# A pipelined first mixer and router, and expert weights streamed per tile as the stationary operand, in a two-layer Flamingo block

## The chip, the cores and the metric

One Trainium2 chip; the kernel runs on one of its cores. The metric is the device time of one execution in microseconds (us). All tensors are float32 unless a row says bf16 or f16.

## What is computed

The input is 2 x 1024 tokens of width 256. Two layers, each a mixer and a mixture of experts, each added to the residual stream behind a tanh gate:

```python
x = x + tanh(g_xattn[0]) * depool_mixer(layernorm(x), ctx)      # rmsnorm, x @ W_in.T + b_in, plus depooled context rows
x = x + tanh(g_ffn[0])   * experts0(layernorm(x))               # 8 experts, top 2, relu, hidden 1024
x = x + tanh(g_xattn[1]) * attention(layernorm(x), ctx)         # 16 heads, 77 context + 1024 own keys
x = x + tanh(g_ffn[1])   * experts1(layernorm(x))               # 32 experts, top 4
# experts1, token t, chosen expert e:
g = x @ w1[e]; u = x @ w3[e]                                    # 256 -> 192
out[t] += weight[t, e] * ((silu(g) * u) @ w2[e])                # 192 -> 256
```

## The kernel before, in words

The residual stream (16 tiles of 128 tokens) stays in SBUF. The program is a sequence of stages, each a block with a program per engine; a block ends only when every engine's program has ended, SP's included. The stages are `prepare`, `depool_mixer`, `router(0)`, `route(0)`, `experts0`, `combine(0)`, then `project_qkv`, `attend`, `project_out`, `router(1)`, `route(1)`, `experts1`, `combine(1)`.

**First mixer and router.** `depool_mixer` takes 16 tiles in turn. For each, ACT normalises it (L552), PE turns it by two transposes (L534), ACT copies the turned tile out of PSUM (L559), PE multiplies by the input weights and adds the context rows with a one-hot matmul (L543, L544), DVE adds the result to the residual (L517), makes a later tile's one-hot (L510) and takes statistics (L522). When all 16 tiles are through, `router(0)` starts: the statistics of all tiles become a scale and a shift (`moments`, L107 to L114, then L605, L585, L586), and each tile is normalised (ACT, L602), stored to HBM for the later gathers (SP, L621), turned (PE, L635), copied (ACT, L615), multiplied by the router weights (PE, L644) and biased (DVE, L592). SP also loads the small weights and the first five of the eight 1 MB W2 matrices during the mixer; the other three and b2 are issued in `route(0)`.

**route(0)** finds the two experts of each token, the softmax weights, and where every token goes. PE and ACT first turn 19 weight blocks that later stages need (`later_turns`, L869 and L742: the attention weights, the second gate, and b1). ACT's exponential for the softmax (L745) stands behind those 19 copies in ACT's program, and DVE waits for it at L801.

**project_qkv** loads early weights of the second experts from POOL's queue: 26 DMAs of 384 KB (W1 and W3 of two experts each, L1553), behind one memset (L1376). **project_out** issues the rest from SP: W1 and W3 of the last six experts (12 DMAs, L1553) and 30 W2 matrices (L1547), 192 KB each. So at the start of `experts1` W1, W3 and W2 of all 32 experts lie in SBUF.

**experts1** runs 95 tiles of up to 128 gathered tokens of one expert. A tile is gathered by POOL's indirect DMA into a ring of four (L901), turned by PE (two transposes, L1109), copied by ACT (L1160). The turned tokens are then the stationary operand and [W1 | W3] is the moving one: two accumulating matmuls of 384 columns (L1115). ACT takes the silu (L1172), DVE multiplies (L1203), giving tokens x 192; PE turns that in two halves of 96 (L1121), ACT copies it (L1166), and two matmuls with 96 contraction rows and 256 columns give the output (L1130), which DVE copies (L1191) and SP stores (L1220). In iteration j, PE does gate and up of tile j, turns the hidden rows of j-1, does down of j-2, and turns the tokens of j+2. A float32 matmul is two records in the trace.

`experts0` (39 tiles) has the other order already: W1 is streamed per tile (1 MB from SP, L969, its expert number read by SP at L966) and is the stationary operand of 16 matmuls of 128 columns (L992).

Of the kernel before, what the change touches and what calls it, by code (L numbers as in the profile page):

```python
# [27 lines left out]
IH = I1 // 2  # L28
# [26 lines left out]
W2_1 = E1 * W13_BYTES  # L55
ARENA = W2_1 + E1 * 2 * D * 4
# [3 lines left out]
W2_TOP = (TOP - W2_1) // (2 * D * 4)  # L60
EARLY = 26
ATT0 = EARLY * W13_BYTES

# [53 lines left out]
def make_env(nc, ctx, a, out):  # L117
# [15 lines left out]
    e.w0_in, e.w13_early, e.w13_in, e.w2_in = (ctx.enter_context(nc.semaphore(n)) for n in ("w0_in", "w13_early", "w13_in", "w2_in"))  # L133
# [62 lines left out]
    e.w13 = carve(0, [E1, DK, 2 * I1])  # L196
    e.w2b = carve(W2_1, [E1, 2, D])

# [258 lines left out]
W2_EARLY = 5  # L457
# [10 lines left out]
def later_turns(e):  # L468
# [8 lines left out]
    turn.append((raw.b1[0:E0 * HK0, :], E0 * HK0, e.b1T))  # L477
# [3 lines left out]
def depool_mixer(e):  # L481
# [5 lines left out]
    U = 4  # L487
    LAG = 3
    xn = e.carve(0, [U, D], base=e.scr)
    xT = e.carve(U * D * 4, [U, DK, P], base=e.scr)  # L490
    oh = e.carve(2 * U * D * 4, [U, P], base=e.scr)

    with nc.Block() as block:
        @block.sync
        def _(sp):
            load_small(e, sp)
            for ex in range(W2_EARLY):
                load_w2_first(e, sp, ex)

        @block.vector  # L500
        def _(dve):
# [12 lines left out]
            for i in range(NTILE + 1):  # L514
                if i < NTILE:
                    dve.wait_ge(mixed_raw, i + 1)
                    v.scalar_tensor_tensor(e.x[:, i, :], ps[:, U + i % U, 0:D], e.tg[:, 0:1], e.x[:, i, :], ALU.mult, ALU.add).then_inc(x_new, 1)  # L517
                if i + U < NTILE:
                    patch(i + U)
                if i >= 1:  # L520
                    dve.wait_ge(x_new, i)
                    v.bn_stats(e.stats[:, i - 1, :], e.x[:, i - 1, :])  # L522

        @block.tensor
        def _(pe):
            for i in range(NTILE + LAG):
                if i < NTILE:
                    pe.wait_ge(xn_ready, i + 1)
                    if i == DEPB:
                        pe.wait_ge(dep_taken, 1)  # L530
                    if i >= U:
                        pe.wait_ge(xT_ready, i - U + 1)
                    for k in range(DK):
                        last = nc.tensor.transpose(ps[:, i % U, k * P:(k + 1) * P], xn[:, i % U, k * P:(k + 1) * P], e.ident[:])  # L534
                    last.then_inc(xT_raw, 1)
                if i >= LAG:
                    j = i - LAG
                    pe.wait_ge(xT_ready, j + 1)
                    pe.wait_ge(oh_ready, j + 1)
                    if j >= U:  # L540
                        pe.wait_ge(x_new, j - U + 1)
                    for k in range(DK):
                        nc.tensor.matmul(ps[:, U + j % U, 0:D], xT[:, j % U, k, :], e.winT[:, k, :], start=(k == 0), stop=False)  # L543
                    nc.tensor.matmul(ps[:, U + j % U, 0:D], oh[0:CL, j % U, :], e.dep[0:CL, j // TPB, :], start=False, stop=True).then_inc(mixed_raw, 1)  # L544

        @block.scalar
        def _(act):
            for i in range(NTILE + 2):
# [4 lines left out]
                if i >= 2:  # L553

                    j = i - 2
                    act.wait_ge(xT_raw, j + 1)
                    if j >= U:
                        act.wait_ge(mixed_raw, j - U + 1)
                    nc.scalar.activation(xT[:, j % U, :, :].rearrange("p k t -> p (k t)"), ps[:, j % U, 0:D], ACT.Copy).then_inc(xT_ready, 1)  # L559
# [88 lines left out]
def route(e, layer):  # L648
# [10 lines left out]
    tr_raw, tr_done = sem(nm + "tr_raw"), sem(nm + "tr_done")  # L659
    turn = later_turns(e) if layer == 0 else []  # L660
    TRB, NTR = 4, 3
# [54 lines left out]
    with nc.Block() as block:  # L716
        if layer == 1:
            @block.sync
            def _(sp):

                for x in range(W2_TOP, E1):
                    load_w2(e, sp, x)

# [15 lines left out]
        def _(act):  # L739
            for n, (src, rows, dst) in enumerate(turn):  # L740
                act.wait_ge(tr_raw, n + 1)
# [1353 lines left out]
```

## Time and profile before

| what | value |
|---|---|
| median of 3 runs | 1420.8 us (1420.45 to 1429.21) |
| profiled execution, its own time | 1419.02 us |
| span of its profile | 1417.2 us |
| mean granted TensorE clock | 0.88 of full |
| busy: PE, PE weight loads, DVE, ACT, POOL | 82%, 50%, 50%, 42%, 23% |
| HBM read and written | 116.5 MB and 30.4 MB |

The profiled execution is one run; its time stands 1.8 us over its span, for what lies outside the first and last instruction, and 1.8 us under the median. PE is TensorE's matmuls, PEld its weight loads, SPq the instructions of SP's queue, and a letter q behind an engine its sequencer.

### The profile page before, as it was taken

What the parts mean: (1) busy time and instruction counts of PE and PEld (TensorE: products, weight loads), DVE (VectorE), ACT (ScalarE), POOL (GpSimd) and SP (SyncE); (2) the same over time, 40 slices, a digit from 0 to 9 for tenths busy, and PEclk for the clock granted to TensorE, in tenths of its full rate; (3) what the DMA queues carried; (4) which work ended last, traced back from release to release, by engine and by line L of the source; (5) the groups of instructions that cost most, each with busy time, mean ns of one, the idle gap of its engine ahead of it and who ended that gap; (6) DMA issues with size and microseconds to landing.
All of it is one profiled execution on the core that took longest, in us unless ns stands there. A gap on an engine that the chain in (4) does not pass through costs nothing. (4 is left out here: it accounts for less than half of the span.)

```text
span 1417.2 us, 25678 instructions
## 1 busy us (share of the span) xinstructions
PE 1158.4 (82%) x6415; PEld 713.4 (50%) x6416; DVE 712.6 (50%) x1862; ACT 594.1 (42%) x1385; POOL 319.4 (23%) x527
## 2 busy tenths in 40 slices
PE   4877999999925969999999999987528999999300
PEld 3767999999923512333333233325515777777200
DVE  6451222222244577888788888824293333333433
ACT  3541221222203505777677777774434333333100
POOL 2003222222106020111101101000003333333475
PEclk9758999999976957999999999999557999999755
DMA  5435555555437743213213123006502333334244
GB/s 170 150 124 202 178 178 184 185 181 185 141 102 228 236 84 48 31 18 49 35 14 47 19 29 47 1 1 149 156 0 64 101 102 100 101 102 99 86 131 115
DMA packets 94693, 147.95 MB, mean 104 GB/s; under 512 B 15399, under 2 KB 71617, under 8 KB 94491
## 3 DMA queue, kind: packets, MB, share of 16 engines
q1 hardware_dynamic: 78026, 103.74, 27.1%
q0 software_dynamic: 14288, 41.30, 9.8%
q10 hardware_dynamic: 2304, 2.10, 0.4%
q8 instruction: 24, 0.39, 0.1%
q14 instruction: 51, 0.41, 0.1%
HBM read 116.52 MB, written 30.38 MB: 104 GB/s over the span
## 5 line engine op out<-in xcount | busy, mean ns | idle before, releaser
L1932 DVE TENSOR_REDUCE arena<-ps 128x1 f32<-128x512 f32 x512 | 328.1, 683 | 73.3 <-PE ps L1773 64.0
L1903 ACT ACTIVATE arena<-ps 128x512 f32<-128x512 f32 (+1 forms) x576 | 304.1, 598 | 142.2 <-PE ps L1814 140.8
L1814 PE MATMUL ps<-arena 99*128 99x512 bf16 (+1 forms) x576 | 217.6, 390 | 6.2 <-ACT arena L1903 5.8
L1773 PE MATMUL ps<-arena 96*128 96x512 bf16 x512 | 206.7, 407 | 13.5 <-DMA arena<-k_parts 11.1
L901 POOL DMA_INDIRECT xg<-xn,tcol x134 | 127.7, 953 | 342.5 <-DVE tcol L934 338.6
L1803 PE MATMUL ps<-arena 128*17 128x512 f32 (+1 forms) x1152 | 154.7, 609 | 2.1 <-ACT arena L1903 1.0
L992 PEld LDWEIGHTS ps<-scratch,arena 128*128 128x128 f32 x1248 | 146.9, 194 | 3.6 <-issue 1.7
L992 PE MATMUL ps<-scratch,arena 128*128 128x128 f32 x1248 | 147.4, 277 | 1.1 <-ACT scratch L1023 1.1
L1814 PEld LDWEIGHTS ps<-arena 99*128 99x128 bf16 (+1 forms) x576 | 57.2, 101 | 181.1 <-ACT arena L1903 139.8
L1005 PE MATMUL ps<-arena,scratch 128*128 x624 | 141.0, 380 | 0.0
L1115 PE MATMUL ps<-arena,scratch 128*128 x380 | 140.0, 492 | 0.2 <-issue 0.2
L1005 PEld LDWEIGHTS ps<-arena,scratch 128*128 128x128 f32 x624 | 115.7, 190 | 14.0
L1062 DVE TENSOR_SCALAR scratch<-ps,arena 128x128 f32<-128x128 f32 x156 | 44.0, 345 | 126.0 <-PE ps L992 125.9
L1023 ACT ACTIVATE scratch<-ps 128x256 f32<-128x256 f32 x39 | 14.9, 383 | 208.8 <-PE ps L983 208.8
L1203 DVE TENSOR_TENSOR scratch<-ps,scratch 128x192 f32<-128x192 f32 x95 | 34.0, 358 | 131.0 <-ACT scratch L1172 131.0
L1130 PE MATMUL ps<-arena,scratch 96*128 x380 | 97.9, 380 | 0.4 <-DVE ysb L1191 0.4
L1773 PEld LDWEIGHTS ps<-arena 96*128 96x128 bf16 x512 | 51.5, 101 | 62.2 <-DVE arena L1932 25.7
L1722 POOL TENSOR_TENSOR scratch<-arena 128x64 f32 (+1 forms) x64 | 18.7, 292 | 266.3 <-DVE arena L1951 252.1
L1115 PEld LDWEIGHTS ps<-arena,scratch 128*128 128x128 f32 x380 | 65.5, 192 | 26.2 <-issue 1.5
L1265 POOL DMA_INDIRECT arena<-y,slot_u x64 | 61.7, 965 | 35.5 <-issue 19.2
L1172 ACT ACTIVATE scratch<-ps 128x192 f32<-128x192 f32 x95 | 31.4, 330 | 88.0 <-PE ps L1115 88.0
L1130 PEld LDWEIGHTS ps<-arena,scratch 96*128 96x128 f32 x380 | 64.6, 190 | 6.0 <-issue 0.9
(290 smaller groups left out, 1304.8 us busy)
## 6 DMA issues: line engine op xcount, KB each, us to landing
arena<-in_L_ffn_W SPq DMA_DIRECT2D x47, 1024.0 KB, 5.0
y<-ysb SPq DMA_DIRECT2D x95, 128.0 KB, 1.7
arena<-in_L_ffn_w POOLq DMA_DIRECT2D x26, 384.0 KB, 10.3
arena<-in_L_ffn_w SPq DMA_DIRECT2D x44, 192.0 KB, 7.0
arena<-k_parts SPq DMA_DIRECT2D x48, 137.6 KB, 4.9
arena<-q_parts SPq DMA_DIRECT2D x96, 64.0 KB, 5.3
xn<-scratch SPq DMA_DIRECT2D x32, 128.0 KB, 1.7
scratch<-y SPq DMA_DIRECT2D x16, 256.0 KB, 2.8
```

What stands on the lines that cost most here:

```text
L901: pool.indirect_dma_start(out=e.xg[:, r, :], out_offset=None, in_=e.xn[layer], in_offset=bass.IndirectOffsetOnAxis(ap=e.tcol[:, r:r + 1], ...
L992: ins = nc.tensor.matmul(chunk(r, n), w1[:, r % 2, k, n * P:(n + 1) * P], xT[:, r % 2, k, :], start=(k == 0), stop=(k == DK - 1))
L1005: last = nc.tensor.matmul(ps[:, YB + r % 2, 0:D], hT[:, r % 2, k, :], e.w2[:, ex, k, :], start=(k == 0), stop=(k == HK0 - 1))
L1062: v.tensor_scalar(hT[:, r % 2, k, :], chunk(r, k), e.b1T[:, bass.ds(ex * HK0 + k, 1)], 0.0, ALU.add, ALU.max).then_inc(high_ready, 1)
L1115: ins = nc.tensor.matmul(ps[:, GB + r % 2, 0:2 * I1], xT[:, r % 2, k, :], e.w13[:, ex, k, :], start=(k == 0), stop=(k == DK - 1))
L1130: last = nc.tensor.matmul(ps[:, YB + r % 2, 0:D], aT[0:IH, r % 2, k, :], e.w2b[0:IH, ex, k, :], start=(k == 0), stop=(k == 1))
L1265: pool.indirect_dma_start(out=yg[:, u, k, :], out_offset=None, in_=e.y[1], in_offset=bass.IndirectOffsetOnAxis(ap=e.slot_u[:, i, k:k + 1], ...
L1773: nc.tensor.matmul(ps[:, MAXB + pos % NMAXB, :], e.q_aug[u][0:QROWS, c, h, t * P:(t + 1) * P], e.k_aug[u][0:QROWS, h, CL + k * HB:CL + (k ...
L1803: ins = nc.tensor.matmul(ps[h * 32:h * 32 + HD + 1, AB, :], e.v_g[u][0:rows, mt, h, :], e.prob[s % 2][0:rows, h, :], start=(mt == 0), stop ...
L1814: nc.tensor.matmul(ps[0:rows, SB + n % NSB, :], e.k_aug[u][0:AROWS, h, k0:k0 + rows], e.q_aug[u][0:AROWS, c, h, :], start=True, stop=True) ...
L1903: nc.scalar.activation(e.prob[s % 2][0:rows, h, :], ps[0:rows, SB + (s * GH + h) % NSB, :], ACT.Exp).then_inc(p_ready, 1)
L1932: v.tensor_reduce(e.mx[:, c, h, t, k:k + 1], ps[:, MAXB + pos % NMAXB, :], AX.X, ALU.max).then_inc(max_done, 1)
```

## The change

Five edits.

1. `depool_mixer` and `router(0)` become one stage, `mix_and_score`. In step s, PE turns tile s, mixes tile s-2, turns the normalised tile s-8 for the router, and scores tile s-10. Statistics become scale and shift in chunks of four tiles. Every PSUM buffer of the stage is double where it was fourfold.
2. 18 of the 19 turns move out of `route(0)` into `combine(0)`; that of b1 stays, its copy behind ACT's exponential. Four W2 matrices are loaded in the first stage, not five.
3. W1 and W3 of the second experts are no longer preloaded. SP loads both for every tile of `experts1` (two DMAs of 192 KB) into a ring of four, with a read of the expert number, and stores the output of tile j-6 behind the loads of tile j.
4. W2 is loaded in `project_qkv` from POOL's queue in 16 DMAs of four experts each, followed by a memset of 32 partitions x 8192 elements; `project_out` and `route(1)` issue no loads.
5. In `experts1`, [W1 | W3] is the stationary operand: three chunks of 128 columns, two matmuls of 128 moving columns each. The hidden rows come out turned, so the two transposes and ACT's copy go. ACT takes the silu in two instructions, DVE multiplies in three. Down has 128 and 96 contraction rows (64 real and 32 zero rows) where it had 96 and 96.

```diff
+def mix_and_score(e):
+    U, R = 4, 8
+    LAG, BEHIND = 2, 2 * CHUNK
+    STATS_AT = CHUNK - 1 + LAG + 1
...
         @block.tensor
         def _(pe):
+            for s in range(STEPS_ALL):
+                i = s
                 if i < NTILE:
                     pe.wait_ge(xn_ready, i + 1)
+                    if i >= 2:
+                        pe.wait_ge(xT_ready, i - 1)
...
+                j = s - LAG
+                if 0 <= j < NTILE:
                     pe.wait_ge(xT_ready, j + 1)
                     pe.wait_ge(oh_ready, j + 1)
...
+                i = s - BEHIND
+                if 0 <= i < NTILE:
+                    pe.wait_ge(zn_ready, i + 1)
...
+                j = s - BEHIND - LAG
...
+                if j >= 0:
+                    pe.wait_ge(zT_ready, j + 1)
...
         @block.scalar
         def _(act):
...
+                if s > STATS_AT and (s - STATS_AT - 1) % CHUNK == 0 and s - STATS_AT - 1 < NTILE:
+                    c = (s - STATS_AT - 1) // CHUNK
+                    act.wait_ge(var_ready, c + 1)
+                    nc.scalar.activation(e.std[:, c * CHUNK:(c + 1) * CHUNK], e.ve[:, c * CHUNK:(c + 1) * CHUNK], ACT.Sqrt).then_inc(std_ready, 1)
+                i = s - BEHIND
+                if 0 <= i < NTILE:
+                    if i % CHUNK == 0:
+                        act.wait_ge(shift_ready, i // CHUNK + 1)
...
 def experts1(e):
+            def load(j, r):
+                ex = sp.value_load(e.expert[0:1, bass.ds(j, 1)], min_val=0, max_val=E1 - 1)
+                if at_least(j, RING1):
+                    sp.wait_ge(gu_raw, (j - RING1) * 2 + 2)
+                for at, name in ((0, "L1_ffn_w1"), (I1, "L1_ffn_w3")):
+                    sp.dma_start(e.w13[:, r, :, at:at + I1], e.a[name][bass.ds(ex, 1)].rearrange("e (k p) i -> p (e k) i", p=P)).then_inc(w13_in[r], 16)
...
-            def gate_up(j, r, ex):
+            def gate_up(j, r, turn):
+                pe.wait_ge(w13_in[r], turn * 32 + 32)
                 pe.wait_ge(xT_ready, j + 1)
-                for k in range(DK):
-                    ins = nc.tensor.matmul(ps[:, GB + r % 2, 0:2 * I1], xT[:, r % 2, k, :], e.w13[:, ex, k, :], start=(k == 0), stop=(k == DK - 1))
-                ins.then_inc(gu_raw, 1)
+                for n in range(3):
+                    for k in range(DK):
+                        ins = nc.tensor.matmul(chunk(r, n), e.w13[:, r, k, n * P:(n + 1) * P], xT[:, r % 2, k, :], start=(k == 0), stop=(k == DK - 1))
+                    if n != 1:
+                        ins.then_inc(gu_raw, 1)
...
             def body(j, r, turn, first, last):
-                dve.wait_ge(silu_ready, j + 1)
+                dve.wait_ge(silu_ready, j * 2 + 2)
                 if at_least(j, 2):
-                    dve.wait_ge(a_turned, j - 1)
-                v.tensor_tensor(act_in[:, r % 2], ps[:, GB + r % 2, I1:2 * I1], silu[:, r % 2], ALU.mult).then_inc(a_ready, 1)
+                    dve.wait_ge(y_raw, j - 1)
+                v.tensor_tensor(hT[0:IB, r % 2, 0, :], chunk(r, 1)[IB:P], silu[0:IB, r % 2, 0, :], ALU.mult)
+                v.tensor_tensor(hT[IB:P, r % 2, 0, :], chunk(r, 2)[0:IB], silu[IB:P, r % 2, 0, :], ALU.mult)
+                v.tensor_tensor(hT[0:IB, r % 2, 1, :], chunk(r, 2)[IB:P], silu[0:IB, r % 2, 1, :], ALU.mult).then_inc(h_ready, 1)
...
-            for ex in range(0, EARLY, 2):
-                load_w13(e, pool, ex, e.w13_early, 2)
+            for ex in range(0, E1, W2_TURN):
+                load_w2(e, pool, ex)
+            nc.gpsimd.memset(e.w2b[IB:IB_PAD, :, 1, :], 0.0)
...
     aT = e.ysb[:].rearrange("p u (k t) -> p u k t", k=DK)
 
     with nc.Block() as block:
-        @block.sync
-        def _(sp):
-            for ex in range(EARLY, E1):
-                load_w13(e, sp, ex, e.w13_in)
-            for ex in range(W2_TOP):
-                load_w2(e, sp, ex)
-
```

## Rows read from the trace of the kernel before

**Rows 1.** Windows; columns: us, busy (x records) of each engine, granted clock, DMA share, GB/s
```profile
core 0: us, PE busy (x) PEld busy (x) DVE busy (x) ACT busy (x) POOL busy (x), PEclk, DMA share, GB/s
...
57.00:77.00 20.00, 19.57 (x96) 18.75 (x96) 2.67 (x16) 12.85 (x31) 0.00 (x0) 0.50 0.31 106
...
1100.00:1300.00 200.00, 200.00 (x926) 142.56 (x925) 64.95 (x231) 77.13 (x231) 72.75 (x77) 1.00 0.34 101
```

**Rows 2.** Timeline, TensorE, one steady tile of experts1; columns: start us, length us
```profile
1202.99 0.38 PE L1109 MATMUL ps<-ident,xg 128*128 128x128 f32 x2
...
1203.22 1.46 PE L1115 MATMUL ps<-arena,scratch 128*128 x4
...
1204.51 0.13 PEld L1121 LDWEIGHTS ps<-ident,scratch 128*96 128x96 f32 x1 [0.20 <-issue]
...
1204.72 1.03 PE L1130 MATMUL ps<-arena,scratch 96*128 x4
...
1205.59 0.38 PE L1109 MATMUL ps<-ident,xg 128*128 128x128 f32 x2
```

**Rows 3.** Timeline of the first mixer and router
```profile
41.30 1.03 PE L543 MATMUL ps<-arena,scratch 128*128 128x256 f32 x4
...
42.82 1.03 PE L543 MATMUL ps<-arena,scratch 128*128 128x256 f32 x4
...
54.22 0.19 DVE L107 TENSOR_TENSOR ln_tmp<-stats 128x16 f32<-128x16 f32 x1 [0.30 <-PEq L493]
...
58.10 0.59 ACT L602 ACTIVATE scratch<-x_resident,shift,rstd 128x256 f32<-128x256 f32 x1
...
58.85 0.59 ACT L602 ACTIVATE scratch<-x_resident,shift,rstd 128x256 f32<-128x256 f32 x1
...
65.09 0.86 PE L644 MATMUL ps<-arena,scratch 128*128 128x8 f32 x4
...
66.26 0.86 PE L644 MATMUL ps<-arena,scratch 128*128 128x8 f32 x4
...
76.76 0.17 DVE L592 TENSOR_TENSOR scratch<-ps,arena 128x8 f32<-128x8 f32 x1 [0.69 <-PE ps L644]
```

**Rows 4.** Timeline: route(0) behind its exponential; a table load of ACT in experts1
```profile
84.52 0.19 DVE L801 TENSOR_REDUCE scratch<-scratch 128x16 f32<-128x32 f32 x1 [2.43 <-ACT scratch L745]
...
1076.22 1.28 ACT L1172 ACT_TABLE_LOAD   x1
```

**Rows 5.** Timeline: end of project_out, begin of router(1)
```profile
984.73 13.95 SPq L1547 DMA_DIRECT2D arena<-in_L_ffn_w  x18
...
991.86 0.75 DVE L2064 BATCH_NORM_STATS2 stats<-x_resident 128x6 f32<-128x256 f32 x2
...
999.13 0.19 DVE L107 TENSOR_TENSOR ln_tmp<-stats 128x16 f32<-128x16 f32 x1 [6.52 <-PEq L2017]
```

**Rows 6.** Timeline, TensorE, one steady tile of experts0
```profile
199.83 3.73 PE L992 MATMUL ps<-scratch,arena 128*128 128x128 f32 x32
...
203.40 0.38 PE L983 MATMUL ps<-ident,xg 128*128 128x128 f32 x2
...
207.07 3.73 PE L992 MATMUL ps<-scratch,arena 128*128 128x128 f32 x32
```

**Rows 7.** Lines 966, 969, 1220, SP's queue: ns min/median/max, first and last start us
```profile
L966 SPq TENSOR_LOAD <-expert x39: 262/267/472, 106.3 to 370.8; - x39
...
L969 SPq DMA_DIRECT2D arena<-in_L_ffn_W x39: 372/373/407, 107.3 to 377.6; - x39
...
L1220 SPq DMA_DIRECT2D y<-ysb x95: 332/332/362, 1084.2 to 1325.7; - x95
```

**Rows 8.** Windows: SP's 192 KB loads of W1/W3 (first two), then of W2 (third)
```profile
972.00:974.00 2.00, 2.00 (x7) 1.56 (x6) 0.00 (x0) 0.87 (x3) 0.00 (x0) 0.51 0.90 249
...
976.00:978.00 2.00, 2.00 (x13) 1.72 (x12) 1.73 (x6) 0.70 (x2) 0.00 (x0) 1.00 1.07 341
...
985.00:990.00 5.00, 4.99 (x27) 4.03 (x24) 5.00 (x15) 1.15 (x3) 0.00 (x0) 1.00 1.13 250
```

**Rows 9.** Timeline: POOL's memset in project_qkv and DVE beside it
```profile
433.21 3.77 POOL L1376 MEMSET arena<- 3x4408 bf16 x1 [31.90 <-POOLq L2074]
...
433.67 3.35 DVE L110 TENSOR_SCALAR mean<-ln_tmp 128x16 f32<-128x16 f32 x1
```

More of the change, by code:

```diff
@@ L546, in _ @@
         @block.scalar
         def _(act):
-            for i in range(NTILE + 2):
+            for s in range(STEPS_ALL):
+                i = s
                 if i < NTILE:
@@ L739, in _ @@
         def _(act):
-            for n, (src, rows, dst) in enumerate(turn):
-                act.wait_ge(tr_raw, n + 1)
-                nc.scalar.activation(dst, ps[:, TRB + n % NTR, 0:rows], ACT.Copy).then_inc(tr_done, 1)
             act.wait_ge(act_in, 1)
@@ L1102, in experts1, with _, store, body @@
         move_tiles(e, 1, block, gathered, tcol_ready)
+        @block.sync
+        def _(sp):
+            def load(j, r):
[4 more added lines that the diff above has]
+                    sp.dma_start(e.w13[:, r, :, at:at + I1], e.a[name][bass.ds(ex, 1)].rearrange("e (k p) i -> p (e k) i", p=P)).then_inc(w13_in[r], 16)
+            def store(j, r):
+                sp.wait_ge(y_ready, j + 1)
+                sp.dma_start(e.y[1][bass.ds(j * P, P), :], e.ysb[:, r, :]).then_inc(y_stored[r], 16)
+            def body(j, r, turn, first, last):
+                load(j, r)
+                if at_least(j, LAG_Y):
+                    store(j - LAG_Y, (r - LAG_Y) % RING1)
+            for j in range(LAG_Y):
+                load(j, j % RING1)
+            turns = (NT1 - LAG_Y) // RING1
+            with sp.Fori(0, turns) as t:
+                for u in range(RING1):
+                    body(t * RING1 + (LAG_Y + u), (LAG_Y + u) % RING1, None, False, False)
+            for j in range(LAG_Y + turns * RING1, NT1):
+                body(j, j % RING1, None, False, False)
+            for j in range(NT1 - LAG_Y, NT1):
+                store(j, j % RING1)
+            for r in range(RING1):
+                sp.wait_ge(y_stored[r], 16 * ((NT1 - 1 - r) // RING1 + 1))
         @block.tensor
@@ L1214, in _ @@
                 out(j, j % RING1, j // RING1)
-        @block.sync
-        def _(sp):
-            def body(j, r, turn, first, last):
-                sp.wait_ge(y_ready, j + 1)
-                sp.dma_start(e.y[1][bass.ds(j * P, P), :], e.ysb[:, r, :]).then_inc(y_stored[r], 16)
-            tile_loop(sp, NT1, RING1, body)
-            for r in range(RING1):
-                sp.wait_ge(y_stored[r], 16 * ((NT1 - 1 - r) // RING1 + 1))
 def combine(e, layer):
@@ L2070, in flamingo_block @@
         attention_buffers(e)
-        for stage, *args in ((prepare,), (depool_mixer,), (router, 0), (route, 0), (experts0,), (combine, 0)):
+        for stage, *args in ((prepare,), (mix_and_score,), (route, 0), (experts0,), (combine, 0)):
             stage(e, *args)
```

234 lines of the change are left out of this document (145 added, 89 removed).

## The prediction

> **What bounds the kernel now.** I read the windows first, to find each stage's engine and clock, then the timeline inside each stage that the change touches, then SP's queue and the DMA windows. From 1100 to 1300 us TensorE is busy 200 of 200 us at the full granted clock, while ACT has 77 us, DVE 65 and the DMA engines a share of 0.34 [rows 1]. So in experts1 only TensorE's own time per tile counts, and what is saved on ACT or DVE is worth nothing. The timeline gives that tile: 1205.59 - 1202.99 = 2.60 us, with no gap: 0.23 turning tokens, 1.29 gate and up (1203.22 to 1204.51), 0.21 turning the hidden rows, 0.87 down [rows 2]. The first mixer is bound the same way, at 42.82 - 41.30 = 1.52 us a tile; the router behind it costs 66.26 - 65.09 = 1.17 us a tile [rows 3], at a granted clock of 0.50, the 1.2 GHz level [rows 1]. Two more places stand still for reasons that are not arithmetic: DVE in route(0) waits 2.43 us for ACT's exponential [rows 4], and router(1) starts 6.52 us after DVE's last statistics, because SP is still issuing weight loads until 984.73 + 13.95 = 998.68 us and the block ends with its last engine [rows 5].
>
> **Experts1, TensorE.** Gate and up become 3 x 2 matmuls of 128 columns, 12 records. The nearest rows are those of experts0, the same form and the same full clock: 32 records from 199.83 to 203.40 us, 3.57 us, or 0.112 us a record [rows 6]. Twelve make 1.34 us where 1.29 stood: the same 768 columns, a little dearer by the weight loads. The hidden turn of 0.21 goes. Down keeps its 2 x 256 columns; I cost 128 and 96 rows in place of 96 and 96 at nothing, since columns set its 0.87 us. New tile: 0.23 + 1.34 + 0.87 = 2.44 us. 95 tiles x 0.16 = 15 us saved, and some 1 us at the end, where one turn, one copy and their waits leave the drain: 16 us.
>
> What is late next? ACT per tile: one copy and two silus, about 1 us by its rate now (77.1 us of work over 77 tiles for three instructions [rows 1]). DVE: three products, a copy and a column; it has 0.84 us a tile now (65 us over 77), and two more instructions of at most 0.4 us leave it under 1.7. The chain from the end of gate and up through silu and products to the next use of the PSUM bank has about two tiles, 4.9 us, for some 2 us of work. PE's new wait for the weights stands ahead of everything in its iteration, down of j-2 and the turn of j+2 included, so lateness there costs in full. Two resources decide it.
>
> *SP.* Per tile it now reads an expert number, issues two loads and one store. From the start of the read to the start of the load is 107.3 - 106.3 = 1.0 us, the load takes 0.37 [rows 7]. Below: the instructions alone, 0.27 + 2 x 0.37 + 0.33 = 1.3 us; above: 1.0 + 2 x 0.5 + 0.5 = 2.5 us with generous register work. I take 2.3, since the read's wait is real: just below 2.44. At 2.5 the tile would be 2.5 and 6 us lost.
>
> *DMA.* Gathers and stores take 0.34 of the engines over 2.6 us [rows 1], 0.88 us a tile. W1 and W3 are 393 KB. The same 192 KB loads from SP ran at 249 GB/s in their first microseconds and then at 341 [rows 8]: 1.58 or 1.15 us. Sum 2.03 to 2.46 us; I take 2.1, because the later window is the steady one. Loads are issued about three tiles (8 us) ahead of use, so their latency is covered; if the cover goes, each tile waits. At the start, SP's first pair is issued about 1.5 us after the block begins while the first gathers take longer: nothing.
>
> A rule speaks against this edit. The Trainium skill, "DMA: Bandwidth & Descriptors", section Bandwidth, wants DMAs batched to 1 MiB or more for three quarters of peak, and gives 138 GB/s for 64 KB. By that rule 192 KB loads would stay well under 341 GB/s. At 200 GB/s, an estimate between that page's two figures, the loads would take 2.0 us, the tile 2.85 and the whole come to 1427. The trace disagrees: queued back to back, 192 KB loads reached 341 GB/s [rows 8].
>
> **First mixer and router.** PE's work is not removed, it is laid together: until now the router starts after the last tile's statistics (moments from 54.22 us) and ends at 76.9 [rows 3]. Start-up is unchanged, as the first mix waits for DVE's one-hot. From about 32 us on steps 4 to 7 are mixer only, 1.52 us each, to 38. Router work in a step costs two transposes, 0.23 at full clock [rows 2], and four score records; at the 1.2 GHz level these come to 0.71 of the 1.17 us, and at the full clock I take 0.112 each [rows 6], 0.45 (bounds 0.45 and 0.71). So steps 8 and 9 take 1.75, steps 10 to 15 2.2, 16 and 17 about 2.0. Each chunk of statistics adds a path DVE, ACT, DVE, ACT before the normalised tile exists: I walk it at some 1.4 us of stall for the first and 0.9 for the two next. That gives 38 + 3.5 + 13.2 + 4 + 3.2 = 62 us. Steps 18 to 25 have no mix and run at ACT's 0.75 us a pair of instructions [rows 3], with a stall of about 1.5 for the last chunk: 62 + 6 + 1.5 = 69.5, and end 70.3 instead of 76.9: 6.5 us saved. If the clock drops to 1.2 GHz when the mixes run out, eight steps cost 1.17: 3.4 us less, so 3. If no stall shows, 10.
>
> **route(0).** ACT's 18 copies no longer stand ahead of the exponential. A table load does not wait for its instruction's semaphore: in experts1 it ran from 1076.22 us, before its silu's input was there [rows 4]. So the exponential is ready when DVE comes and the whole 2.43 us go; 1.1 if the load came late. In combine(0) the moved turns run on PE and ACT, idle there beside DVE's sums: nothing; 5 us if the sums waited, which no wait in the code makes them do. The fourth W2 load, issued in route(0) in place of the mixer, has some 30 us until the first expert.
>
> **project_qkv and project_out.** The loads leave SP, so router(1) starts 6.2 us earlier (6.52 less the 0.3 that a block costs [rows 3, 5]). Router(1)'s own clock I leave at its lower level. POOL's new memset has 8192 elements a partition; at the 3.77 us for 4408 [rows 9] it takes 7.0 us, from about 449 us. DVE's tensor_scalar beside the old one took 3.35 us, held up by it [rows 9]. DVE's work at that time reads PSUM, so I take nothing; at most the 7 us. The Trainium skill, "SBUF — State Buffer", describes a port pair shared by VectorE and GpSimd as an exclusive lock for the whole instruction; the trace agrees for that one pair (3.35 us for 128x16 elements), and by the rule products with a PSUM input are free of it.
>
> **Sum.** 16 + 6.5 + 2.4 + 6.2 = 31 us off the profiled execution's 1419.0: 1388 us. It stands 1.8 below the median of the runs shown, inside what I can tell, so I leave the figure at 1388.
>
> **Rivals.**
> *A. SP or the DMA queue sets the tile* at 2.5 to 2.75 us, mostly by the 249 GB/s row together with late gathers. For it: both sums above lie within 0.4 us of 2.44. Against: a ring of four. Time at 2.6: 1388 + 15 = 1403; at 2.75: 1418.
> *B. Streaming starves TensorE: slower than before.* The W2 loads from the same queue held only 250 GB/s at a saturated share of 1.13 [rows 8]. Should W1/W3 rows, with gathers and stores in between, cost what those did, the loads take 1.58 x 1.13 / 0.90 = 2.0 us and with the 0.88 and a wait per tile for a late gather of some 0.3 the tile is 3.2: (3.2 - 2.44) x 95 = 72, so 1460. It decides from 2.44 + 31/95 = 2.77 us a tile. The batching rule named above speaks for this rival; the 341 GB/s window speaks against it.
> *C. The pipelined stage gains nothing,* since two-deep buffers make PE, ACT and DVE wait for each other in every step: 1388 + 6.5 = 1394. For: each step has four waits on PE; against: ACT needs 1.5 of 2.2 us, DVE about 1.7.
> *D. More goes than I count:* with 6 us less idle time ahead of router(1) its clock stays at 2.4 GHz, tiles at 0.75 to 0.8 instead of 1.17 us: 6 us more, 1382; with the stall-free first stage 1378.
>
> **How the numbers follow.** Forecast 0.58, A 0.14, B 0.05, C 0.13, D 0.10. The range 1376 to 1410 takes D, C and most of A and leaves out B. About 1% (14 us) is what a measurement of this kernel can tell from no change. Faster by over 1% (under 1406.6): forecast, C, D and half or more of A, 0.90; within 1%: the rest of A, 0.05; slower: B, 0.05.
>
> **What would show it.** In the profile after: PE's steady tile in experts1 2.44 us with PE busy throughout and a DMA share of 0.8 to 0.9; the last score of the first router at about 70 us; no idle time ahead of L801's successor; router(1)'s moments within 0.5 us of project_out's last statistics. A PE wait for the DMA of W1/W3 or the gather would be A or B; a tile over 2.77 us makes the prediction wrong in sign.

## The result, and the profile after

The changed kernel takes 1413.72 us (median of 9 runs, 1410.21 to 1417.34) where the kernel before, timed beside it, takes 1425.71 (9 runs, 1415.46 to 1429.21): a ratio of 0.992, 95% interval 0.990 to 0.995. That is 12 us faster, outside the predicted 1376 to 1410 and well short of the 31 us of the sum. The profiled execution took 1411.37 us, its span 1409.6.

| stage, profiled execution | before | after |
|---|---|---|
| first mixer and router end | 76.93 | 69.71 |
| route(0) | 28.88 long | 26.36 long |
| router(1) begins | 999.1 | 980.4 |
| from route(1)'s end to experts1's end | 256.4 | 256.1 |
| combine(1), unchanged code | 87.5 long | 98.8 long |

experts1's end is the issue of its last store, combine(1) runs from its first instruction to the issue of its last output store; both are taken so in every run below.

Windows: the stretch of the first router, two short ones inside it, and experts1 (they answer to [rows 1]). The router's stretch is short and at the full clock until 65.3 us, at 0.50 from there on. In experts1 TensorE is no longer busy all the time: 213.26 of 220 us, and the DMA share has gone from 0.34 to 0.87.

```profile
57.00:70.00 13.00, 10.65 (x67) 9.88 (x66) 4.32 (x22) 7.05 (x19) 0.00 (x1) 0.82 0.25 82
...
64.00:66.00 2.00, 1.74 (x13) 1.58 (x13) 0.33 (x2) 1.82 (x5) 0.00 (x0) 0.82 0.39 131
66.00:68.00 2.00, 2.00 (x11) 2.00 (x11) 0.33 (x2) 0.77 (x3) 0.00 (x0) 0.50 0.39 131
...
1080.00:1300.00 220.00, 213.26 (x1525) 192.94 (x1524) 115.25 (x425) 78.82 (x254) 78.29 (x83) 1.00 0.87 251
```

Timeline, the end of the first router (it answers to the last lines of [rows 3]): the last scores are written at 69.54 + 0.17 us.

```profile
68.69 0.17 DVE L574 TENSOR_TENSOR scratch<-ps,arena 128x8 f32<-128x8 f32 x1 [0.69 <-PE ps L614]
69.54 0.17 DVE L574 TENSOR_TENSOR scratch<-ps,arena 128x8 f32<-128x8 f32 x1 [0.69 <-PE ps L614]
```

Timeline of route(0) and of router(1)'s begin (they answer to [rows 4] and [rows 5]). L882 is the reduction that waited 2.43 us for the exponential; it waits for nothing now. L109 is router(1)'s first instruction; the 6.52 us ahead of it have become 0.30.

```profile
74.64 0.22 DVE L877 TENSOR_TENSOR scratch<-scratch 128x128 bf16<-128x128 bf16 x1
74.78 0.18 DVE L882 TENSOR_REDUCE scratch<-scratch 128x16 f32<-128x32 f32 x1
...
979.41 0.74 DVE L2160 BATCH_NORM_STATS2 stats<-x_resident 128x6 f32<-128x256 f32 x2
...
980.46 0.19 DVE L109 TENSOR_TENSOR ln_tmp<-stats 128x16 f32<-128x16 f32 x1 [0.30 <-PEq L2120]
```

Timeline, TensorE in experts1: two tiles without hindrance (1200.85, 1203.28 and 1205.70 us), and one with it. They answer to [rows 2].

```profile
1107.70 0.38 PE L1221 MATMUL ps<-ident,xg 128*128 128x128 f32 x2
1107.92 1.51 PE L1229 MATMUL ps<-scratch,arena 128*128 128x128 f32 x12
1109.27 1.03 PE L1239 MATMUL ps<-arena,scratch 128*128 x4
1110.14 0.38 PE L1221 MATMUL ps<-ident,xg 128*128 128x128 f32 x2
1110.44 1.60 PE L1229 MATMUL ps<-scratch,arena 128*128 128x128 f32 x12
...
1200.85 0.38 PE L1221 MATMUL ps<-ident,xg 128*128 128x128 f32 x2
1201.07 1.50 PE L1229 MATMUL ps<-scratch,arena 128*128 128x128 f32 x12
1202.41 1.03 PE L1239 MATMUL ps<-arena,scratch 128*128 x4
1203.28 0.38 PE L1221 MATMUL ps<-ident,xg 128*128 128x128 f32 x2
...
1205.70 0.38 PE L1221 MATMUL ps<-ident,xg 128*128 128x128 f32 x2
```

A tile takes 2.43 us, with 0.22 for the turn, 1.34 for gate and up and 0.87 for down: the predicted 2.44. At 1110 us gate and up begin 0.30 after the turn instead of 0.22, and between 1080 and 1290 us 27 of 80 tiles lose time in this place, up to 1.3 us each and 10.1 us in all. Over tiles 9 to 85 the mean, taken from the starts of ACT's copies (L1265), is 2.605 us. The kernel before had a steady 2.597. Nothing is gained there.

Lines 1188, 1192 and 1196 show what SP does for one tile: read an expert's number, issue two loads and a store. Columns: ns min/median/max, first and last start.

```profile
L1188 SPq FUSED_REGOPS  x161: 16/152/284, 1051.5 to 1294.4; - x161
L1188 SPq TENSOR_LOAD <-expert x95: 58/269/636, 1051.2 to 1294.2; - x95
...
L1192 SPq DMA_DIRECT2D arena<-in_L_ffn_w x190: 3/381/726, 1052.0 to 1295.3; - x190
...
L1196 SPq DMA_DIRECT2D y<-ysb x95: 99/368/464, 1067.1 to 1306.7; - x95
```

The four big instructions make 0.27 + 2 x 0.38 + 0.37 = 1.4 us. The load instructions of tiles 9 to 85 follow one another at a mean of 2.597 us, so 1.2 us a tile are register work and the gaps between instructions. In means: 0.93 us from the start of the read to that of the first load, 0.50 to the second load, 0.58 to the store and 0.60 to the next read, a quarter of the loop's branch in it. SP's mean is TensorE's mean, and the weights arrive just in time: between 1080 and 1290 us the first product of gate and up starts within 0.25 us of the last recorded landing on its slot in 56 of 80 tiles.

### The profile page after: what moved, and what is told of

Its sections match the earlier page's. It is cut to its first block and busy times, and to the rows that moved or that the text cites. A ratio compares the mean times of both kernels' runs of the same rounds, so it can differ in the third digit from the quotient of the medians.

```text
span 1409.6 us, 27573 instructions
## 1 busy us (share of the span) xinstructions
PE 1139.0 (81%) x6984; PEld 749.1 (53%) x6986; DVE 763.1 (54%) x2071; ACT 587.2 (42%) x1388; POOL 320.2 (23%) x518
## 5 line engine op out<-in xcount | busy, mean ns | idle before, releaser
L2035 DVE TENSOR_REDUCE arena<-ps 128x1 f32<-128x512 f32 x512 | 327.6, 682 | 69.7 <-PE ps L1876 59.5
L1229 PE MATMUL ps<-scratch,arena 128*128 128x128 f32 x1140 | 147.8, 280 | 6.1 <-DMA arena<-in_L_ffn_w 3.6
L1071 PEld LDWEIGHTS ps<-scratch,arena 128*128 128x128 f32 x1248 | 147.9, 195 | 3.6 <-issue 1.7
L1071 PE MATMUL ps<-scratch,arena 128*128 128x128 f32 x1248 | 148.4, 278 | 1.1 <-ACT scratch L1102 1.1
L1229 PEld LDWEIGHTS ps<-scratch,arena 128*128 128x128 f32 x1140 | 136.4, 194 | 12.6 <-issue 11.7
L1084 PE MATMUL ps<-arena,scratch 128*128 x624 | 141.0, 379 | 0.0
L1084 PEld LDWEIGHTS ps<-arena,scratch 128*128 128x128 f32 x624 | 115.6, 190 | 14.1
L1102 ACT ACTIVATE scratch<-ps 128x256 f32<-128x256 f32 x39 | 14.9, 383 | 209.9 <-PE ps L1062 209.9
L1239 PE MATMUL ps<-arena,scratch 128*128 (+1 forms) x380 | 97.9, 380 | 0.7 <-DVE ysb L1289 0.7
L1301 DVE TENSOR_TENSOR scratch<-ps,scratch 64x128 f32<-64x128 f32 x95 | 27.8, 293 | 114.5 <-PE ps L1239 89.6
L1265 ACT ACTIVATE scratch<-ps 128x256 f32<-128x256 f32 x95 | 36.4, 383 | 84.8 <-issue 55.0
L1239 PEld LDWEIGHTS ps<-arena,scratch 128*128 128x128 f32 (+1 forms) x380 | 65.2, 191 | 6.1 <-issue 1.1
```

Of the source, the lines that this page charges most:

```text
L1071: ins = nc.tensor.matmul(chunk(r, n), w1[:, r % 2, k, n * P:(n + 1) * P], xT[:, r % 2, k, :], start=(k == 0), stop=(k == DK - 1))
L1084: last = nc.tensor.matmul(ps[:, YB + r % 2, 0:D], hT[:, r % 2, k, :], e.w2[:, ex, k, :], start=(k == 0), stop=(k == HK0 - 1))
L1229: ins = nc.tensor.matmul(chunk(r, n), e.w13[:, r, k, n * P:(n + 1) * P], xT[:, r % 2, k, :], start=(k == 0), stop=(k == DK - 1))
L1239: last = nc.tensor.matmul(ps[:, YB + r % 2, 0:D], hT[0:rows, r % 2, k, :], e.w2b[0:rows, ex, k, :], start=(k == 0), stop=(k == 1))
L2035: v.tensor_reduce(e.mx[:, c, h, t, k:k + 1], ps[:, MAXB + pos % NMAXB, :], AX.X, ALU.max).then_inc(max_done, 1)
```

## The experiments

Times are medians; each ratio is against the kernel before, timed in the same job. "Mean tile" is that of tiles 9 to 85 as above. A job is one batch of kernels timed together on one chip. There were five, and the kernel before has a median of its own in each: 1425.0 us beside again, store_act, half_w13 and sum_unrolled; 1423.4 beside half_store, sum_both, first_only and second_only; 1425.4 beside before_again, before_third, no_pad and best_stream; 1416.6 beside best_gather, best_simple, out_unrolled and before_sum; 1416.6 beside again_third and best_gather_again. So ratios are compared rather than times.

**What holds experts1's tile.** `again` is the changed kernel once more.

> The changed kernel as it is, once more. Two parts of its profile are in question: experts1's tile at a mean of 2.60 us instead of 2.43, and combine(1), which took 98.8 us instead of 87.5 although its code is unchanged, with 27 register instructions of DVE at some 0.7 us each. If both belong to the kernel, the time is again 1414 (within 4 us), the tile 2.60 and combine(1) 96 to 100 us. If the stall in combine(1) belonged to that one execution, combine(1) takes 87 to 89 us here and this run lies at 1400 to 1405.

1410.35 us, ratio 0.990 (0.986 to 0.993). Mean tile 2.594: it came back. combine(1) took 94.7 us, under the 96 to 100 I expected but far from 87.5.

`store_act`: the y stores leave SP's program and stand in ACT's, behind its copy_x.

```diff
-                if at_least(j, LAG_Y):
-                    store(j - LAG_Y, (r - LAG_Y) % RING1)
...
+                if at_least(j, 3):
+                    store(j - 3, (r - 3) % RING1)
```

> The y stores of experts1 leave SP's queue for ACT's. Theory S (SP's program, some 2.4 us a tile and 3.1 on every fourth, sets the mean of 2.60): without its third DMA, some 0.5 us a tile, SP needs about 2.1 and TensorE's own 2.43 is the mean, so experts1 takes 16 us less and the time is 1397 to 1401. Theory D (the DMA engines, busy share 0.87, cannot move 393 KB of weights, a gather and a store faster than 2.6 us): the bytes are the same, so the mean stays at 2.58 to 2.62 and the time at 1412 to 1416.

1398.98 us, ratio 0.981 (0.978 to 0.984), a time inside Theory S's range. But the mean tile is 2.505: neither 2.43 nor 2.60. The waits of SP's queue from 1100 to 1250 us say more than the time: in `again` that view is empty, SP never waited in 58 tiles. Here it waits 59 times for TensorE to free a slot.

```profile
SPq L1192 <- PE ps L1219: 27.2, 59, 1.3
```

So SP's program was the limit in the changed kernel. It would now do with 2.505 - 27.2 / 59 = 2.04 us a tile, and something else holds the tile. The weights no longer come late: of 84 tiles none starts gate and up within 0.25 us of a landing.

`half_w13`: the same instructions, half of the bytes (the second 128 input rows of W1 and W3 are left out).

```diff
-  sp.dma_start(e.w13[:, r, :, at:at + I1], e.a[name][bass.ds(ex, 1)]...)
+  sp.dma_start(e.w13[:, r, 0:1, at:at + I1], e.a[name][bass.ds(ex, 1), 0:P]...)
```

> Every load of W1 and W3 brings only its first 128 input rows, so half of the bytes and packets, with SP's instructions unchanged (the second half of the ring's weights is never loaded, so the second layer's experts use other numbers there). Theory S (SP's program sets the tile): mean tile 2.58 to 2.62 still, time 1412 to 1416. Theory D (DMA engines): the loads need half of the time, the mean falls to 2.43, and the time to 1397 to 1401.

1395.55 us, ratio 0.979 (0.976 to 0.982), mean tile 2.49. Neither theory forecast this mean, and the edit did not separate them as I meant it to. The waits of SP's queue are empty again, so SP is still the limit, but at 2.509 us a tile where `again` had 2.590. Most of these 0.08 us are the issue itself, shorter for a load of half the rows: a median of 0.34 and 0.38 us for the two loads of a tile, where the full ones took 0.36 to 0.37 and 0.41. TensorE's mean is another 0.02 lower than SP's. The halved loads also land 1.8 us after their issue instead of 3.6 to 3.9 (medians), so part of SP's lead could be used up; that this gives the 0.02 is not shown.

`half_store`: both edits.

> Both earlier edits of experts1 at once: the y stores on ACT's queue and only the first 128 input rows of W1 and W3 loaded. With either alone the mean tile fell from 2.59 to 2.50 (stores moved) and 2.49 us (bytes halved). Theory S2: two limits lie close together, SP's program at 2.5 to 2.6 us a tile (in the run with half of the bytes SP still waits for nothing and runs at 2.51) and behind it the time that a load takes to land once its slot is free (in the run with the stores moved SP waits 0.48 us a tile for the slot). Then both edits together reach TensorE's own 2.43 us, experts1 ends 5 us earlier than in either, and the time is 1390 to 1393. If instead TensorE's own occasional stalls make up the rest, the mean stays at 2.49 to 2.50 and the time at 1396 to 1399.

Mean tile 2.429, TensorE busy 180.00 of 180 us, experts1 240.2 us long where `store_act` had 248.7 and `half_w13` 245.3: there were two limits and no third. That the second was the landing of the weights, as S2 says, is refuted by `best_stream` below. The whole time of 1397.7 us (ratio 0.981, 0.977 to 0.984) missed its figure: the attention, whose code is the same, took 469.0 us where it took 465.0 in `store_act`'s profile. TensorE's clock stood at 0.50 for its first 45 us here and for its first 37 in `store_act`. Over all profiles, of either kernel, the attention took 464.5 to 465.7 or 467.8 to 469.2 us, and once 466.8.

`best_stream`: eight slots for W1 and W3 (`R13 = 8`; SP's and TensorE's loops unrolled by eight), stores on ACT, combine's loops written out.

> A version meant to beat both: y stores on ACT's queue, a ring of eight slots for W1 and W3 (over the attention's space, which is free by then) with all loops of SP and TensorE unrolled by eight, and combine(1)'s loops written out. If the stalls that are left with the stores moved (mean tile 2.505) come from a load landing late after its slot was freed, a ring twice as deep covers them and the mean tile is 2.43: experts1 takes 239 to 241 us, and with combine(1) at 89 us the time is 1384 to 1388. If the DMA engines are simply full (share 0.89 at 2.50 us), a deeper ring gives nothing: the mean stays at 2.48 to 2.51, experts1 at 246 to 248 us and the time at 1391 to 1395.

1399.15 us, ratio 0.982 (0.978 to 0.986), 4 us over the higher of the two ranges. Mean tile 2.498, no better than four slots. The ring of weights was not the second limit, and neither were full engines, as the next run shows. The idle times over 0.1 us of TensorE's weight loader from 1080 to 1290 us stand mostly at L1209, the turn of gathered tokens: 7.3 us in 21 tiles, against 2.4 at gate and up.

`best_gather`: eight places for gathered tokens too.

```diff
-    gathered = [sem(f"e1_gathered{r}") for r in range(RING1)]
+    gathered = [sem(f"e1_gathered{r}") for r in range(R13)]
...
-                    token_column(e, dve, j + RING1, r, tcol_ready)
+                    column(j + R13, r)
```

> As best_stream (stores on ACT's queue, eight slots for W1 and W3, combine's loops written out), and eight places for gathered tokens as well, so that a gather is asked for eight tiles ahead of its use instead of four. In best_stream TensorE's remaining waits, some 7 us between 1080 and 1290 us, stand at the turn of gathered tokens. If a gather has too little lead while the weights keep the DMA engines at a share of 0.91, twice the lead brings the mean tile to 2.43 (experts1 239 to 242 us) and the time to 1390 to 1394. If the engines are simply full, the waits come back at the weights and the mean stays at 2.49 to 2.51, experts1 at 247 to 249 us, the time at 1396 to 1401.

1388.42 us, ratio 0.981 (0.978 to 0.983), in a job where before stood at 1416.6. Mean tile 2.429, experts1 242.0 us. Windows, 1100 to 1280 us:

```profile
1100.00:1280.00 180.00, 180.00 (x1337) 168.55 (x1336) 100.39 (x371) 69.09 (x223) 66.15 (x70) 1.00 0.93 261
```

The DMA engines are busier than in any other run, 0.93, and TensorE never waits. They were not full at 0.87 or 0.91. The gather was asked for too late for its longer way under load. In the kernel before, with only gathers and stores on the engines, a gather landed a median 2.7 us after its issue; here and in `best_stream` it takes 4.5 to 4.6, in `half_store`, where the tile was 2.43 too, 3.0. And a ring of four does not give four tiles of lead, as I had written. In `best_stream` a gather goes out some 5 us before its turn, two tiles, since its issue comes two tiles after its place is free: DVE writes the column behind the next tile's products. With eight places it is 14.5 us. The turn starts within 0.25 us of the gather's last recorded landing in 23 of 84 tiles of `best_stream` and in none of this run.

`best_simple`: stores on ACT and combine's loops written out, four slots.

> Only two edits on the changed kernel: y stores on ACT's queue and combine's loops written out (DVE's loop is shared by both layers' stages, so combine(0)'s too), ring of four kept. Against best_stream it tells whether the ring of eight does anything: experts1 took 247.9 us with four slots and 248.2 with eight. Alone, the edits gave 11 and 9 us over the changed kernel; they sit in different stages, so together 18 to 20: 1390 to 1394, experts1 at 247 to 249 and combine(1) at 89 to 90 us. If best_stream's 1399 is what such a combination really gives, it is 1396 to 1400.

1393.35 us, ratio 0.984 (0.981 to 0.988), mean tile 2.49, experts1 246.7. Four slots do as well as eight, as long as the gather has four.

`best_gather_again`, in another job:

> The best version once more (y stores on ACT's queue, eight slots for W1 and W3 and for gathered tokens, combine's loops written out), in another job. TensorE's mean tile is 2.43 us again, experts1 241 to 242 us and combine(1) 89 us, so 1387 to 1394 whatever before does; the ratio is 0.980 to 0.981 where before stands at 1416, and 0.974 to 0.977 where it stands at 1424.

1390.67 us, ratio 0.982 (0.980 to 0.984), mean tile 2.43, combine(1) 89.4. This is the version to keep: 14.5 us faster than the changed kernel beside it (`again_third`, 1405.15).

**The padded rows.** `no_pad`: the second chunk of inner rows with its own 64 rows.

```diff
-IB_PAD = 96
+IB_PAD = IB
...
-            v.memset(hT[IB:IB_PAD, :, 1, :], 0.0)
...
-            nc.gpsimd.memset(e.w2b[IB:IB_PAD, :, 1, :], 0.0)
```

> The changed kernel with the second chunk of inner rows at its own 64 rows instead of 96, so without the two memsets of the pad. If the rows of the stationary operand cost nothing, the second down product keeps its time (columns set it), TensorE's unhindered tile stays at 2.43 us and the time at 1410 to 1414, with perhaps 1 us less in project_qkv, where POOL's memset falls away. If 64 rows made TensorE slower (lower clock or another weight load), the tile would be 2.5 or more on its own and the granted clock between 1100 and 1280 below 1.00; then 1415 to 1425.

1430.99 us, ratio 1.004 (1.001 to 1.006): neither expectation, for the clock is 1.00 and the tile is slow all the same. TensorE is busy throughout and a tile takes 2.77 us:

```profile
1199.83 0.44 PE L1221 MATMUL ps<-ident,xg 128*128 128x128 f32 x2
1200.10 1.50 PE L1229 MATMUL ps<-scratch,arena 128*128 128x128 f32 x12
1201.44 1.22 PE L1239 MATMUL ps<-arena,scratch 128*128 x4
1202.59 0.44 PE L1221 MATMUL ps<-ident,xg 128*128 128x128 f32 x2
```

Down spans 1.15 us (1201.44 to 1202.59) where it spanned 0.87, the turn 0.27 for 0.22. The weight loads by shape show how, in no_pad first and in the changed kernel second (columns: busy us, mean ns, idle before, releaser):

```profile
L1239 PEld LDWEIGHTS ps<-arena,scratch 64*128 64x128 f32 x130 | 19.1, 184 | 21.5 <-issue 21.5
L1221 PEld LDWEIGHTS ps<-ident,xg 128*128 128x128 f32 x130 | 13.1, 140 | 21.5 <-issue 21.5
```

```profile
L1239 PEld LDWEIGHTS ps<-arena,scratch 96*128 96x128 f32 x138 | 26.4, 191 | 3.5
L1221 PEld LDWEIGHTS ps<-ident,xg 128*128 128x128 f32 x136 | 19.1, 141 | 7.1
```

A load of 64 rows takes no longer, but TensorE's loader stands idle ahead of the 64-row loads and ahead of the first load after them: 43 us over 65 tiles, where it had 10.6 over 69. In one tile's records the first 64-row load starts 0.31 us after the product ahead of it has started; the 96-row load starts with that product. So the 32 rows of zeros are worth 0.34 us of TensorE's own tile. Beside the changed kernel, whose tile SP holds at 2.60, they are worth 0.17 us a tile, 16 us in all, and they are what makes this change a gain.

**The first half and the second half alone.** `first_only` is the kernel before with the merged mixer and router and the moved turns; `second_only` the changed kernel with the first stages of before.

> The kernel before with the first half of the change alone: first mixer and router as one pipeline, the turns moved from route(0) to combine(0). The profile of the changed kernel shows 7.2 us less at the end of the first router, 2.5 less in route(0), 1.1 lost again in experts0 and up to 0.6 in combine(0): 8 to 10 us faster than before, 1415 to 1417 where before lies at 1425. combine(1) takes 87 to 88 us if its stall belongs to the other half, 95 to 99 if it comes from this one.

> The changed kernel with the first stages of before: only experts1 (stationary and streamed weights) and the loads taken from project_out and route(1). From the profile: 6 us won between project_out and router(1), nothing in experts1 (tile 2.60 as before), and combine(1) 7 to 11 us longer if its stall belongs to this half: 1426 to 1430 where before lies at 1425. If the stall belongs to the first half or to the placement of the code as a whole, combine(1) takes 87 us and the time is 1418 to 1420.

`first_only`: 1416.84 us, ratio 0.995 (0.992 to 0.998); route(0) ends at 97.5 instead of 106.1 us. `second_only`: 1418.10, ratio 0.994 (0.991 to 0.997); router(1) starts 0.3 us behind project_out, experts1 takes what it took before (256.6 us from route(1)'s end). The two gains, 7 and 8 us by their ratios (each within 4 us), add up to 0.989, the 0.990 to 0.992 of the whole. And combine(1) took 95.2 and 97.3 us, in either half. `second_only` missed the time that I gave for a stall in its half, 1426 to 1430: in this job the kernel before had the stall too, as the next runs make likely.

**combine(1).** The 11.3 us lost there in the profile lie in DVE's own instruction stream. Lines 1296 (before) and 1387 (after) are the same address arithmetic:

```profile
L1296 DVEq ALU_OP  x52: 40/40/40, 413.4 to 1413.5; - x52
```

```profile
L1387 DVEq ALU_OP  x52: 1/40/724, 404.7 to 1405.8; - x52
```

The waits in combine(1), before and after. The products waited for their gathers alone; now they also wait 28.5 us for "issue", nothing that another engine did, and POOL, which sets the stage, waits 9.6 us for DVE to free its buffers.

```profile
DVE x_resident L1297 <- DMA arena<-y,slot_u: 53.8, 16, 4.4
```

```profile
DVE x_resident L1388 <- DMA arena<-y,slot_u: 34.6, 9, 5.4
DVE x_resident L1388 <- issue: 28.5, 15, 5.1
...
POOL arena L1356 <- DVE x_resident L1388: 9.6, 2, 5.9
```

`sum_unrolled`, then `sum_both`: DVE's loop, then ACT's as well, become Python loops (`for t in range(TURNS)` for `with dve.Fori(0, TURNS) as t`). DVE's loop is also combine(0)'s.

> combine(1)'s loop on DVE is written out (no loop branch, no address arithmetic in registers). If DVE's slow register instructions cost combine(1) the 11 us, it takes 87 us again or a little less (its gathers by POOL then set it), and the time is 1402 to 1405. If the stage is long for another reason (the gathers themselves slower, or POOL), it stays at 96 to 99 us and 1414. The tile of experts1 stays at 2.60 under every theory.

> combine(1)'s loops are written out on DVE and on ACT. With DVE's alone written out, DVE's register instructions of 0.7 us were gone, but 23 of ACT's took 0.7 us, and the stage took 92.8 us. If the slow register instructions are the whole of it, none is left here and the stage takes 87 to 88 us as in the kernel before: 1399 to 1402. If something else slows the engines' sequencers (a shared source of instructions), plain instructions without registers are slow too and the stage stays at 92 to 95 us: 1405 to 1410.

`sum_unrolled`: 1405.60, ratio 0.986 (0.983 to 0.988); the stage took 92.8 us, and 23 of ACT's register instructions took 0.7 us. `sum_both`: 1401.49, ratio 0.984 (0.981 to 0.987), none left. The stage took 89.4 us, not the 87 to 88 expected; with both loops written out it took 89.0 to 89.5 in five other profiles, `before_sum`'s among them.

`before_again` and `before_third` asked whether this is the change's doing.

> The kernel before, once more. Its profiled execution had no slow register instruction in combine(1) and took 1419.0 us, while its median over all runs so far is 1423 to 1426. Five other kernels that share combine(1)'s code, the first half of the change alone and the second half alone among them, all have 16 to 40 such instructions at 0.7 us and a stage of 94.7 to 98.8 us. If the stall is no part of the change, it appears here too: combine(1) 94 to 98 us and a profiled time of 1424 to 1430; then 7 to 11 us of the missing gain are a matter of the one execution on which the prediction was built. If the kernel before is free of it, combine(1) takes 87.5 us again and the time is 1417 to 1421.

> The same again, to have three executions of the kernel before beside each other. Stall common to all: combine(1) 94 to 98 us; stall absent from the kernel before: 87.5 us in both; stall by chance: one of each.

The kernel before has it: combine(1) 95.7 and 95.3 us, and L1296 now with a maximum of 709 ns:

```profile
L1296 DVEq ALU_OP  x52: 1/40/709, 413.7 to 1415.4; - x52
```

Their times, 1420.96 and 1426.04, only partly fit the 1424 to 1430 that I expected. Three more runs asked for the condition.

> The kernel before with combine's loops written out on DVE and ACT, nothing else changed. Two of three executions of the kernel before had the slow register instructions (combine(1) 95.7 and 95.3 us), the one profiled first had none (87.5 us). If they are no part of the change, writing the loops out gains the kernel before as much as the changed one: combine(1) at 88 to 90 us, 6 to 9 us faster, 1416 to 1419 where before lies at 1425. If the kernel before mostly runs without them, it gains 0 to 2 us: 1422 to 1426.

> The changed kernel with only ACT's loop of combine(1) written out, DVE's kept. If the slow register instructions come wherever one engine loops in this stage, DVE has again 16 to 40 of them at 0.7 us and the stage takes 94 to 99 us. If it takes two looping engines, DVE's are gone as well and the stage takes 88 to 90 us.

> The changed kernel a third time, timed beside before in one job. Seven profiles of combine(1) with DVE's loop kept had its slow register instructions in three jobs (stage 94.7 to 98.8 us), two had none (the first profile of before, and the changed kernel with ACT's loop written out, in a job where before's median was 1416.6 instead of 1423 to 1425). If they come and go with the job and not with the kernel, the ratio to before is the same as so far, 0.990 to 0.992, whichever level before has here: 1410 to 1414 beside 1423 to 1425, or 1402 to 1406 beside 1416. If the changed kernel has them more often than before, the ratio where before stands at 1416 is 0.995 or above.

`before_sum`: 1416.57 us beside 1416.59, ratio 1.001 (0.999 to 1.004). `out_unrolled`: 1404.51, combine(1) 88.0, no slow instruction on DVE. `again_third`: 1405.15, ratio 0.992 (0.989 to 0.995), the unchanged loops on both engines and still none, combine(1) 88.6 us. These three ran in the two jobs in which before stood at 1416.6. `out_unrolled` therefore says nothing about ACT's loop, and `before_sum` found nothing to remove. `again_third` settles the question that matters: the ratio of 0.990 to 0.992 is the same in jobs with the slow instructions and without. All ten profiles with a loop in combine(1) from three of the jobs have them, of either kernel; the two such profiles from the other two jobs have none. One chip served a job with them and one without, so they do not belong to the chip. That they come with the job is what these twelve profiles suggest, one or a few per job; what brings them is open.

## Why the prediction was wrong

*Experts1, TensorE: right.* 2.44 predicted, 2.43 measured, in every unhindered tile. ACT and DVE never set it. Costing the 96 rows at nothing was right too, but my reason, that columns set the 0.87 us, does not hold in general: at 64 rows, which I would have costed at nothing as well, the tile is 0.34 us longer.

*Experts1, SP: the term that failed.* The sum's largest term, 16 us, rested on SP's program being shorter than TensorE's tile. I took 2.3 us a tile between bounds of 1.3 and 2.5, and called 2.5 generous. SP needs 2.60, above my upper bound. The 1.0 us from the read to the first load was right (0.93 measured). The rest, 1.3 us in the sum for two loads and a store and 1.5 at the bound, was 1.67: 0.50, 0.58 and 0.60 us, the last with its share of the loop's branch. With the tile at SP's 2.60 in place of 2.44 the 15 us of this edit were gone; experts1 gave 0.3 us instead of 16. That was rival A, which I gave 0.14, at the 2.6 us for which it stated 1403. It named SP first but put the time mostly on the slow DMA rate and on late gathers, and neither set it.

*Experts1, DMA: size about right, its consequence missed.* I took 2.1 of 2.44 us, a share of 0.86; at 2.43 us the share is 0.93, or 2.26 us. An estimate for W1 and W3 themselves: going from all bytes (0.93) to half (0.66) at the same tile frees 0.27 x 2.43 = 0.66 us for 197 KB, so 1.3 us for the 393 KB, 300 GB/s. My two rows gave 1.15 and 1.58. The batching rule of the Trainium skill ("DMA: Bandwidth & Descriptors", section Bandwidth), by which such loads would fall well short of that, does not hold for loads queued behind one another here. What I missed is that a transfer can suffer long before the engines are full: the gather was late at a share of 0.89. I had written late gathers into rivals A and B, with 0.3 us a tile; once SP was out of the way they cost 0.07.

*Rival B, starvation: wrong.* No tile mean of a kernel with the pad came near 2.77. The one kernel that did was `no_pad`, for quite another reason.

*First mixer and router: the end is right, partly by luck.* Predicted end 70.3, measured 69.7. The last mix ended at 59.9 where my walk had 62. From there the router took 9.8 us where I had 8.3, because the clock fell to 0.50 at 65.3 us, with the last four tiles still to score. I had priced such a drop at 3.4 us for all eight. Rival C falls.

*route(0): right.* 2.5 us for 2.4.

*The turns in combine(0): not free.* I had them at nothing. The stage took 22.6 to 24.5 us in nine profiles with the moved turns and DVE's loop, 22.3 to 22.5 in four without them: 0.2 to 2.1 us, about 1.

*project_out: right.* The 6.5 us ahead of router(1) became 0.3. In this profile project_out's own work took 1.4 us longer (23.0 for 21.6), so 4.8 of the 6.2 us show; in the two other profiles of the changed kernel it took the 21.6. POOL's longer memset did no harm that shows. Rival D's clock did not come: router(1) takes 22.8 us as before.

*The base: one execution.* I subtracted from one profiled execution, 1419.0, which was fast: the kernel before has a median of 1425.7 beside the changed one. In that execution combine(1) took 87.5 us, and the next profile had 98.8 there. Ratios over many runs are free of this; a sum against one execution is not.

Stage by stage the two profiles differ by 7.6 us. Gains: 7.2 first mixer and router, 2.5 route(0), 1.5 project_qkv, 4.3 attention (unchanged code), 4.8 project_out, 0.3 experts1. Losses: 1.7 experts0 and combine(0), which I had at nothing, and 11.3 combine(1). The forecast of 1388 comes to the measured 1413.7 within 1 us by corrections taken from this profile: 15.7 for SP in experts1, 6.7 for the base, 1.7 for experts0 and combine(0) and 1.4 for project_out, less 0.8 that the first stages gave more. SP's term alone gives 1404, inside the stated range; the base and the small terms took the time out of it.

## What to carry to other kernels

Before a stream is put on a queue engine, count its whole program per turn, register arithmetic and branch included: each DMA with an address from a register cost 0.5 us or more here, not the 0.37 of its own row. A queue that feeds the busy engine and never waits in the waits view is the first suspect for the limit. When a second stream joins, look at the other transfers' lead in the trace, which need not be the depth of their ring, as well as at the engines' share. And look at the same stage in several executions before subtracting from one of them.

## What was not expected of the hardware

- A matrix product with 64 rows in the stationary operand, between products of 128, made the next weight loads stand behind the product ahead instead of beside it: 2.77 us a tile instead of 2.43 with 96 rows, at the full clock. Other forms than this one were not tried.
- A program's register instructions, 0.04 us otherwise, took 0.7 us each in combine(1), 16 to 37 of them within 20 to 66 us, on DVE or, with DVE's loop written out, on ACT; they were there in three of the five jobs and absent in two.
- With the DMA engines at a share of 0.93 and 261 GB/s for 180 us, TensorE waited for nothing.
- Under this load a gather took 4.5 us from issue to landing instead of 2.7, and the 192 KB loads landed some 4 us after their issue.
